# A two-layer graph block on one core: 2 KB runs for the turned blocks, new engine orders, and the K matrix made in two other steps

## The reference

```python
h = jnp.maximum(_layernorm(x, axis=-1), 0.0)
z_l = jnp.einsum('bnd,ed->bne', h, W_lang)
z_g = jnp.einsum('bnd,ed->bne', h, W_grav)
v = jnp.einsum('bnd,ed->bne', h, W_V)
zn = z_l / jnp.maximum(jnp.linalg.norm(z_l, axis=-1, keepdims=True), EPS)
A_l = jnp.maximum(jnp.einsum('bnd,bmd->bnm', zn, zn), 0.0) * not_eye
sq = jnp.sum(z_g * z_g, axis=-1, keepdims=True)
d2 = jnp.maximum(sq + jnp.swapaxes(sq, -1, -2) - 2.0 * jnp.einsum('bnd,bmd->bnm', z_g, z_g), 0.0)
A_g = jnp.exp(-d2 / (2.0 * sigma * sigma)) * not_eye
K_l = _row_stochastic_causal(A_l, causal_mask)   # causal_mask is adj
K_g = _row_stochastic_causal(A_g, causal_mask)
K = w_l * K_l + (1.0 - w_l) * K_g
x = x + jnp.einsum('bne,de->bnd', jnp.einsum('bnm,bmd->bnd', K, v), W_O)
h = jnp.maximum(_layernorm(x, axis=-1), 0.0)
x = x + (jnp.einsum('bnf,nm->bmf', h, adj * adj) + bias)
```

## Time and profile before

| | |
|---|---|
| runs | 1283.26, 1283.47 (median), 1283.98 us |
| the profiled execution | 1283.45 us, its span 1281.7 us, mean granted TensorE clock 0.991 |
| busy | PE 1226.2 us (96%), DVE 1079.5 (84%), ACT 695.6 (54%), POOL 620.9 (48%) |
| DMA | 145.09 MB in 353,536 packets, of which 274,800 under 512 B |

### The profile page before, as it was taken

The page is one execution under the profiler, slowest core; times in us unless marked ns, Lnnn a source line. Parts: engine busy times, 40 slices in busy tenths (PEclk is TensorE's granted clock), DMA queues, the critical chain, the costliest instruction groups (busy, mean ns, idle before and its releaser), DMA issues.

```text
span 1281.7 us, 22765 instructions
## 1 busy us (share of the span) xinstructions
PE 1226.2 (96%) x6076; PEld 1017.4 (79%) x6076; DVE 1079.5 (84%) x1892; ACT 695.6 (54%) x1324; POOL 620.9 (48%) x991
## 2 busy tenths in 40 slices
PE   7998999999999999999999999999999999999995
PEld 7876788887788888788888778888878888877883
DVE  5577888888888888888888888888888888888778
ACT  5355455565555556555556555555655555655543
POOL 1112654644564554565464456455456546445535
PEclk9998999999999999999999999999999999999997
DMA  7222444444444444443444443444454344444302
GB/s 259 56 80 61 108 98 115 128 121 127 123 99 110 118 127 122 136 106 98 115 127 122 127 120 100 110 121 127 121 137 106 97 116 127 122 127 106 83 25 99
DMA packets 353536, 145.09 MB, mean 113 GB/s; under 512 B 274800, under 2 KB 306672, under 8 KB 353520
## 3 DMA queue, kind: packets, MB, share of 16 engines
q1 hardware_dynamic: 352944, 144.57, 41.3%
q10 hardware_dynamic: 576, 0.33, 0.1%
HBM read 62.46 MB, written 49.87 MB: 88 GB/s over the span
## 4 chain that ended last, share of the span: by engine, by line
issue 46%; POOL 36%; PE 8%; DVE 4%; POOLq 2%; SPq 2%; ACT 1%; DMA 1%; ACTq 0%; DVEq 0%
POOL x_ring L323 13%; POOL h_lo L338 7%; PE ring L916 6%; POOL ln L313 5%; POOL rn L344 2%; POOL ln L311 2%; SPq L243 2%; POOL ln L307 1%; POOL ln L301 1%; POOL ln L305 1%; PE p_ps L966 1%; POOL ln L306 1%; PE ring L1011 1%; POOL ln L309 1%; POOL ln L303 1%
## 5 line engine op out<-in xcount | busy, mean ns | idle before, releaser
L338 POOL TENSOR_TENSOR h_lo<-h2f,h_hi 128x512 fp32r<-128x512 f32 x124 | 156.5, 1291 | 332.4 <-ACT h_hi L496 332.2
L916 PE MATMUL ring<-hT_hi,Lw_hi 128*128 128x512 f32 x640 | 253.8, 397 | 14.2 <-DVE x_ring L680 6.8
L916 PE MATMUL ring<-hT_lo,Lw_hi 128*128 128x512 f32 x640 | 250.5, 391 | 0.0
L916 PE MATMUL ring<-hT_hi,Lw_lo 128*128 128x512 f32 x640 | 250.4, 391 | 0.0
L577 DVE TENSOR_TENSOR y_lo<-ring,y_hi 128x512 fp32r<-128x512 f32 x256 | 164.7, 681 | 55.2 <-ACT y_hi L429 55.2
L916 PE MATMUL ring<-MT_hi,hT_hi 128*128 128x512 f32 x512 | 199.4, 389 | 1.4 <-DVE MT_lo L577 1.4
L916 PE MATMUL ring<-MT_lo,hT_hi 128*128 128x512 f32 x512 | 199.2, 389 | 0.0
L916 PE MATMUL ring<-MT_hi,hT_lo 128*128 128x512 f32 x512 | 199.2, 389 | 0.0
L323 POOL TENSOR_TENSOR x_ring<-x_ring,bias_sb 128x512 f32 (+1 forms) x124 | 184.7, 1522 | 3.8 <-ACT h2f L489 3.8
L466 ACT ACTIVATE v_hi<-ring 128x512 fp32r<-128x512 f32 x128 | 75.3, 589 | 193.7 <-PE ring L916 193.7
L916 PEld LDWEIGHTS ring<-hT_hi,Lw_hi 128*128 128x128 f32 x640 | 120.7, 189 | 53.2 <-DVE x_ring L680 18.8
(11 more groups left out here) (165 smaller groups left out, 2605.5 us busy)
## 6 DMA issues: line engine op xcount, KB each, us to landing
x_ring<-in_x SPq DMA_DIRECT2D x32, 1024.0 KB, 5.0
out<-x_ring SPq DMA_DIRECT2D x128, 256.0 KB, 2.2
h_turned<-h SPq DMA_DIRECT2D x496, 64.0 KB, 2.1
p_dram<-chain SPq DMA_DIRECT2D x62, 256.0 KB, 2.1
h<-p_dram SPq DMA_DIRECT2D x248, 64.0 KB, 1.9
rn_cols<-rn_dram SPq DMA_DIRECT2D x31, 256.0 KB, 3.9
x_ring<-in_L_gnn_W_lang SPq DMA_DIRECT2D x4, 256.0 KB, 5.6
h2f<-in_L_gnn_W_grav SPq DMA_DIRECT2D x1, 1024.0 KB, 9.1
```

The source lines that it names most:

```text
L338: pool.tensor_tensor(h2[1][:, b], h2f[:, b], h2[0][:, b].bitcast(F32), ALU.subtract)\
L916: mm = pe.matmul(out, lhsT, rhs, start=(k == 0), stop=(k == len(terms) - 1))
```

## The change

Three parts.

1. `h` and `h_turned` get the layout [partition, block, batch, c, 32], so that what a DMA of `turn_h` moves is one run of 512 floats (2 KB) in each of 32 partitions, on both sides. Before it was 16 runs of 32 floats in each. ACT's and DVE's instructions on `h`, `h_turned` and `hT` take the strides instead; their element counts stay.
2. `K`: ACT runs eight instructions of 128x128 instead of four, and DVE one addition of 128x512 instead of four `scalar_tensor_tensor` of 128x128.
3. Orders. DVE: all four `stats` and all four `add` stand ahead of the v stage, with the squared norms split up among them, and the two `turn_p` are apart. ACT: `h2_full` stands inside the v stage, and `shift` one batch later. POOL: `add_bias` first, behind a wait for `a_ready`, then `h2_lo`, `norm1` of group i+2, `norm2`, and `row_norms`. SP: the first `store_p` before the norms' store, and `rn_cols` after the first four fetches.

```diff
@@ layout
-        h = sb("h", [P, GB, D])
+        h = sb("h", [P, NQ, GB, C, Q])
-        h_turned = sb("h_turned", [P, GB, C, P])
+        h_turned = sb("h_turned", [P, NQ, GB, C, Q])
-            return h_turned[j * Q:(j + 1) * Q, :, :, i * Q:(i + 1) * Q].rearrange("p b c q -> p (b c) q")
+            return h_turned[j * Q:(j + 1) * Q, i].rearrange("p b c q -> p (b c q)")
@@ sync
             def spread_norms_turn_p(g):
+                store_p(g, 0)
                 sp.wait_ge(rn_step, RN_STEPS * g + 1)
                 sp.dma_start(rn_dram, rn[:, 0]).then_inc(rn_stored, 16)
+                store_p(g, 1)
+                fetch_p(g, 0)
                 sp.wait_ge(rn_stored, 16 * g + 16)
                 sp.dma_start(rn_cols[:, :, :], rn_dram.unsqueeze(0).to_broadcast([P, P, GB])).then_inc(rn_spread, 16)
-                store_p(g, 0)
-                store_p(g, 1)
-                fetch_p(g, 0)
                 fetch_p(g, 1)
@@ gpsimd, iteration
-                if after:
-                    norm1(i + 1)
                 if lag:
+
+                    pool.wait_ge(a_ready, 2 * i)
+                    for b in range(GB):
+                        add_bias(i - 2, b)
                     for b in range(GB):
                         h2_lo(i - 2, b)
-                    for b in range(GB):
-                        add_bias(i - 2, b)
+                if after and x_next:
+                    norm1(i + 2)
+                if before and after:
+                    norm2(i - 1)
                 row_norms(i)
@@ scalar, v stage
-                    if b == 0 and after:
+                    if b == 1 and after:
                         shift(i)
+                    if before and after:
+                        for k in {0: [], 1: [0], 2: [1, 2], 3: [3]}[b]:
+                            h2_full(i - 1, k)
@@ scalar, w_g_K_g
                 for b in range(GB):
+                    act.activation(A[:, b, 0], A[:, b, 0], ACT.Copy, scale=deg[:, 3, b, 0:1])
                     e = act.activation(K[:, b], A[:, b, 1], ACT.Copy, scale=deg[:, 3, b, 1:2])
@@ vector, K·v stage
-                squared_norms(i)
                 if before:
+                    dve.wait_ge(drained, use + G_USES + 2)
+                    wait_for(dve, ln2_step, LN_STEPS * (i - 1))
                     add(i - 1, 2, n + 2)
+                    stats(i - 1, 0)
+                    stats(i - 1, 1)
+                    dve.wait_ge(drained, use + G_USES + 3)
                     add(i - 1, 3, n + 3)
+                    stats(i - 1, 2)
+                    dve.wait_ge(drained, use + G_USES + GB)
+                    diagonal(i, 0)
+                    stats(i - 1, 3)
+                    squares(i, 0)
+                    diagonal(i, 1)
+                    squares(i, 1)
+                else:
+                    squared_norms(i)
@@ vector, combine
-                for b in range(GB):
-                    e = dve.scalar_tensor_tensor(out=K[:, b], in0=A[:, b, 0], scalar=deg[:, 3, b, 0:1],
-                                                 in1=K[:, b], op0=ALU.mult, op1=ALU.add)
-                e.then_inc(k_ready, 1)
+                dve.tensor_tensor(K[:, :, :], A[:, :, 0], K[:, :, :], ALU.add).then_inc(k_ready, 1)
```

More of the change, by code:

```diff
@@ L346, in row_norms, with iteration @@
                 pool.tensor_tensor(wr[:, :, :], rn_lg, w8[:, :, :], ALU.mult).then_inc(rn_step, 1)
-            def iteration(i, before=True, lag=True, after=True):
-                if after:
-                    norm1(i + 1)
+            def iteration(i, before=True, lag=True, after=True, x_next=True):
                 if lag:
+                    pool.wait_ge(a_ready, 2 * i)
+                    for b in range(GB):
+                        add_bias(i - 2, b)
                     for b in range(GB):
                         h2_lo(i - 2, b)
-                    for b in range(GB):
-                        add_bias(i - 2, b)
+                if after and x_next:
+                    norm1(i + 2)
+                if before and after:
+                    norm2(i - 1)
                 row_norms(i)
-                if before:
+                if before and not after:
                     norm2(i - 1)
@@ L362, in _ @@
             norm1(0)
+            norm1(1)
             pool.wait_ge(scalars, 9)
@@ L366, in _ @@
             iteration(1, lag=False)
-            with pool.Fori(2, NG - 1) as i:
+            with pool.Fori(2, NG - 2) as i:
                 iteration(i)
+            iteration(NG - 2, x_next=False)
             iteration(NG - 1, after=False)
@@ L407, in normalize @@
                 for b in range(b0, b0 + GB // 2):
-                    act.activation(h[:, b], x_rows(g, b), ACT.Relu, bias=ln1[:, SHIFT, b:b + 1],
+                    rows, out = x_rows(g, b), h_rows[:, b]
+                    if not isinstance(g, int) or g > 0:
+                        rows, out = rows.rearrange("p (c j q) -> p j c q", c=C, j=NQ), h[:, :, b]
+                    act.activation(out, rows, ACT.Relu, bias=ln1[:, SHIFT, b:b + 1],
                                    scale=ln1[:, RSTD, b:b + 1]).then_inc(h_ready, 1)
@@ L471, in iteration @@
                         w_g_K_g(i)
-                    if b == 0 and after:
+                    if b == 1 and after:
                         shift(i)
+                    if before and after:
+                        for k in {0: [], 1: [0], 2: [1, 2], 3: [3]}[b]:
+                            h2_full(i - 1, k)
                 if not after:
                     kt_copy(i)
-                if before:
                     for b in range(GB):
                         h2_full(i - 1, b)
-                        if not after:
-                            h2_copy(i - 1, b)
+                        h2_copy(i - 1, b)
             def h2_full(g, b, last=False):
@@ L742, in iteration @@
                     n += 1
-                    if before and b == 0:
-                        dve.wait_ge(drained, use + G_USES + GB)
-                        wait_for(dve, ln2_step, LN_STEPS * (i - 1))
                     turned_lo(i + 1, b)
-                    if before and b < GB // 2:
-                        stats(i - 1, 2 * b)
-                        stats(i - 1, 2 * b + 1)
-                    if b == 1:
-                        turn_p(i, 0)
-                        turn_p(i, 1)
+                    if b < 2:
+                        turn_p(i, b)
                 if lag:
```

51 lines of the change are left out of this document (30 added, 21 removed).

## The result

The changed kernel takes **1295.74 us** (median of 4 runs, 1294.51 to 1296.68), the kernel before 1283.45 us beside it: a ratio of 1.0095, 95% interval 1.0077 to 1.0112. It is slower by 12.3 us. The prediction was 1291.5, slower. The profiled execution took 1294.51 us; its span grew from 1281.7 to 1292.8 us at a granted clock of 0.993 (before 0.991).

The account below looks back on a forecast made before the run. PE was taken to bound the kernel, with 1.6 us of waiting in each iteration, all in layer 1. 1283.45 + 14.8 (loop) - 5.0 (before it) - 1.7 (last iteration) = 1291.5 us; range 1236 to 1306.

Parts of the forecast that it names:

- the row factors beside POOL: POOL's additions beside the row factors hold DVE's small instructions: they end at T + 11.87 instead of 9.68, 2.2 us lost.
- the sum of +8.1 us: Whole forecast against the kernel before: +14.8 us in the loop, -5.0 before it, -1.7 in the last iteration.
- the issue time of the turned blocks: SP's 16 DMA issues: 0.36 us from one start to the next, 5.8 us instead of 10.7, blocks some 5 us earlier.
- Rival 1: The collision of POOL's additions with the row factors is off the path: 1.25 us less an iteration, 1240.5 us; chance 0.22.
- rival 2: Only the two products of the row factors are held, the `max` not: an iteration 37.1 us, 1253 us; chance 0.12.
- rival 3: The reciprocal of the row factors is held as well: an iteration 39.7 us, 1329 us; chance 0.11.
- K: From row factors to the end of `KT_lo`: 9.87 us instead of 9.06; ACT's scalings +1.18, DVE's combine -0.46.
- The period: From one y stage's start to the next: 38.42 us against 37.91, +0.51, over 29 iterations +14.8 us.
- The tail: The last iteration has no `add_bias` beside `diag`: -1.7 us (0 to -3).
- the prologue: Before the loop: early blocks and idle POOL cut iteration 2's halt from 4.46 to 2.3 us at full clock: -5.0 us.
- Rival 4: The turned blocks' issues stay 0.67 us apart, blocks land at K0 + 9.3, ACT's chain ends 1.15 us later: 1325 us; chance 0.05.
- The tipping point: The sign turns where the row factors take about 1.7 us more than before, given 29 x 1.25 + 6.7 us gained elsewhere.

## Why the prediction was right, and where it was off

The ratio's sign came out of the term on which the prediction rested, the row factors beside POOL. The margin was thin: the sum of +8.1 us is 0.28 us an iteration. That the size is right to 4 us is partly luck: the issue time of the turned blocks, which was off by three quarters, costs little at the place where it stands.

- **Row factors beside POOL.** Predicted end T + 11.87, measured 623.52 - 611.77 = 11.75. The first product, the `max` and the last product held, the reciprocal not (0.202 to 0.204 us in all 32): the turns are as written, with POOL at T + 7.92 instead of 7.85. Rivals 1, 2 and 3 each deny one of these and fall. The reciprocal was never held, 0.203 us; this agrees with the Trainium skill (page "SBUF — State Buffer", section "Who interferes with whom"), whose list of the instructions that GpSimd can block has no reciprocal. Moving the additions away gave back 56.7 us, and putting them into the kernel before cost 57: the collision is shown, from both sides.
- **Rival 1's number** was 1240.5 us for a kernel without the collision. The run that takes it away measured 1239.0. That they agree so well is partly luck: the periods gave (37.88 - 36.44) x 29 = 41.8 us and not 36.3, and the rest about 2 and not 6.7.
- **K.** Predicted 9.87 us from the row factors to the end of `KT_lo`; it is 9.75 (623.52 to 633.27; `KT_lo` starts at 632.59 and lasts 0.68). With 11.87 it made 21.74, which the sum has as 21.72; PE starts K·v at T + 21.63.
- **The period** was predicted 38.42. It is 38.46 in this iteration and 38.42 in the mean. The 37.91 of before was one iteration as well, its mean is 37.88; 29 periods add 0.55 x 29 = 16.0 us instead of 14.8.
- **The tail** was to give 1.7 us and gave 1.6 (1292.8 - 1226.45 = 66.35 from the y stage of iteration 31 to the end, before 1281.7 - 1213.77 = 67.93), with `diag` at 0.681 us in the median and `sqc` at 0.171, as forecast.
- **The step that failed is the issue time of the turned blocks.** I took 0.36 us from one start to the next by the nearest row, the stores of 2 KB rows to DRAM, with 10.7 us for 16 as the upper bound. It is 0.63, near that bound: 10.04 us for the sixteen. The piece did not decide it. So the blocks land at K0 + 8.44, and my "no longer awaited" is wrong: hT_hi waits 2.1 us. That it costs so little follows from what the prediction had on ACT's chain: the run with early blocks shows 16.60 us for the v stage (I had 16.70), with late ones 16.83. The strides, for which I took zero, cost ACT nothing: `hT_hi` has a mean of 626 ns in either layout.
- **In the prologue** the same miss shows, and a second one. I had -5.0 us, with a halt of 2.3 and the full clock. The y stage of iteration 2 starts 1.9 us earlier (110.34, before 112.22), its halt is 2.94:

```profile
110.34 0.78 PE L942 MATMUL ring<-hT_hi,Lw_hi 128*128 128x512 f32 x1 [2.94 <-DVE hT_lo L611]
```

  The clock granted in the 18 us from that start is 0.91, where it was 0.84. The windows, in the same form as above, are of the kernel before, the changed kernel and the run with 8 transfers:

```profile
112.20:130.20 18.00, 17.98 (x73) 0.84 0.11 29
```

```profile
110.30:128.30 18.00, 17.96 (x82) 0.91 0.10 29
```

```profile
108.80:126.80 18.00, 17.96 (x82) 0.91 0.10 32
```

  The last one has a halt of 2.16 us, near my 2.3, and still not the full clock. So the full clock failed by itself, and not for the late blocks alone. I had it from the start of iteration 1, where the halt is 2.13 us and the clock 1.00; the length of the halt alone doesn't tell.

  The y stage of iteration 31 in the kernel before and in the changed one:

```profile
1213.77 0.47 PE L916 MATMUL ring<-hT_hi,Lw_hi 128*128 128x512 f32 x1 [0.32 <-DVE x_ring L680]
```

```profile
1226.45 0.47 PE L942 MATMUL ring<-hT_hi,Lw_hi 128*128 128x512 f32 x1 [0.33 <-DVE x_ring L692]
```

  From iteration 2 to there the changed kernel takes 1226.45 - 110.34 = 1116.1 us, the one before 1213.77 - 112.22 = 1101.6: +14.6, and not the 16.0 of 29 periods, so 1.4 us more come from elsewhere, most of it probably from the better clock (an estimate from the two windows: 0.07 of 18 us, 1.3 us). That makes -3.3 us for the prologue instead of -5.0. The spans differ by 11.1 us (1292.8 - 1281.7), where the sum had 8.1: 1.7 from the prologue, 1.2 from the period, 0.1 from the tail. The profiled execution took 1294.51 us, 1.2 less than the median; with these 3.0 it makes the 4.2 between forecast and result.
- **Rival 4** had the right place and nearly the right price. "The issues stay at 0.67" is not what happened (0.63), but the run with the old layout is that case: I gave 1325, it is 1317.6. What I did not see is how steep it is between: 0.04 us an issue is 0.6 us at the last block, and at this point all of it counts, while the 4 us that I had hoped for below it would have brought 0.23. The Trainium skill (page "DMA: Bandwidth & Descriptors", section "Why small descriptors are slow (HBM only)") says that SBUF-to-SBUF transfers don't suffer from small pieces. From issue to landing the trace agrees, 2.1 us with small pieces and 2.0 with long runs. That the longer runs would therefore bring nothing is not so: they bring 0.04 us an issue, and 21.8 us in all.
- **The tipping point.** I wrote that the sign turns where the row factors take 1.7 us more. My own terms give 1.9 (2.19 less 8.1 / 29). The measured ones give about 1.6: 2.05 us of holding, and 12.3 / 29 = 0.42 us too much in an iteration.

What each part of the change is worth, in an iteration, by the mean periods: the layout -0.7 (39.12 to 38.42), K in its new form +0.7 as long as `KT_lo` is awaited (37.69 to 38.42; nothing to be seen otherwise), the additions beside the row factors +2.0 (36.44 to 38.42). The new orders of DVE and ACT were not run by themselves. Two runs come near: the kernel before with the collision and the changed kernel with the old layout have it both, and their blocks come at the same place (hT_hi at 9.15 and 9.14 us behind K·v). From K·v on the old orders take 18.32 us and the new ones 17.53, so the orders of the v stage are worth 0.79 us together. Besides, `sum_s` starts 4.30 us into the iteration in the run with the old layout (622.18 to 626.48), where it was 5.04 before.

## What to carry to other kernels

Before moving work of GpSimd, look at what VectorE does in that stretch, and count its small instructions, those with two inputs and `tensor_scalar` ones: here each of three was held for up to one GpSimd instruction, so four that need 0.7 us took 2.8. Price a change of a step by whether it is awaited there: the same new K cost 22 us with the collision and nothing that could be measured without it. And where the releaser that a profile names for a wait would make the next edit worthless, test it by moving it: two events that fall together can't be told apart in one trace. Where an edit changes halts of PE, read the granted clock behind them in every iteration, not in one.

## What was not expected of the hardware

- A DMA from SBUF to SBUF took 0.59 to 0.60 us on SP's queue to issue, whether it moved 32 x 2 KB, 64 x 2 KB or 128 x 512 bytes, and 0.63 with 512 x 128 bytes; stores of 128 x 2 KB to DRAM took 0.32.
- The `max` against a constant, with one input of 8 elements a partition, was held for a whole GpSimd addition, as forecast from `sqc` (1.21 us in the median instead of 0.17). Not expected: with two of the four additions gone it was held as long as before (1.214), so half of the additions still cost 1.25 of the 2.05 us.
- Behind halts of 4.46, 2.94 and 2.16 us at the start of iteration 2 the clock granted in the next 18 us was 0.84, 0.91 and 0.91; behind one of 2.13 at the start of iteration 1 it was 1.00 in 16 us. In the run with 8 transfers it fell behind three halts of 1.76 to 2.04 us ahead of K·v, and stayed at 1.00 behind one of 1.50.
